# Layer 2's second fetch pass in a graph network kernel: four sums to a PSUM bank, a ring of 48 fetched tiles, and the node stage spread over three blocks

## The reference

```python
# layer 2, second relational convolution (per edge: its source's message in its relation)
msg = h[etype, src]                                   # rows of a table of node x relation
mean = segment_sum(msg, dst*8+etype) / max(cnt, 1)    # so each edge has a coefficient
x = x + mean.sum(over relations) + h @ root2 + b2
# layer 3, per node, before its edges are walked
nodes = relu(layernorm(x))
q = nodes @ Wq + bq ; k = nodes @ Wk + bk ; v = nodes @ Wv + bv
```

## Time and profile before

| What | us |
|---|---|
| median of three runs | 6053.4 |
| profiled execution, first to last instruction | 7221.2 |
| POOL busy in it | 4096.8 |
| TensorE busy | 4312.1 |
| VectorE busy | 3856.8 |
| this stage's fetches, first issue to last | 4527.5 to 5708.4 |
| the next stage's first fetch | 5748.0 |

### The profile page before, as it was taken

How to read it: one execution, slowest core, us unless ns; L and a number is a source line. 1 busy time by engine, 2 the same in 40 slices (tenths; PEclk the granted TensorE clock), 3 DMA queues, 4 the chain that set the end, 5 groups by cost and what they waited for, 6 DMA issues and landing times. The chain is left out here.

```text
span 7221.2 us, 86037 instructions
## 1 busy us (share of the span) xinstructions
PE 4312.1 (60%) x19030; PEld 3495.4 (48%) x19030; DVE 3856.8 (53%) x11927; ACT 1462.0 (20%) x3928; POOL 4096.8 (57%) x4194
## 2 busy tenths in 40 slices
PE   4577777846656565795666666333344446556565
PEld 4466666635555555443444444233333345555554
DVE  7344444446666556745555555244444446556665
ACT  4122222212222222361111111000000112222222
POOL 1566666646666565006666665666666556555653
PEclk9877767666666666897888888555655566676766
DMA  2433333323333334164444445122222433333333
GB/s 49 125 99 101 100 100 101 100 89 105 106 108 108 105 108 87 64 279 140 130 136 128 136 129 117 52 55 61 59 56 59 72 100 107 110 113 105 113 115 64
DMA packets 426871, 738.64 MB, mean 102 GB/s; under 512 B 100571, under 2 KB 280628, under 8 KB 419797
## 3 DMA queue, kind: packets, MB, share of 16 engines
q0 software_dynamic: 173296, 436.67, 23.0%
q1 hardware_dynamic: 244484, 289.62, 12.3%
q10 hardware_dynamic: 8592, 6.82, 0.4%
HBM read 613.74 MB, written 120.20 MB: 102 GB/s over the span
## 5 line engine op out<-in xcount | busy, mean ns | idle before, releaser
L1619 POOL DMA_INDIRECT xh<-pair_d,src_i x1658 | 1653.2, 997 | 1181.9 <-issue 457.1
L2630 POOL DMA_INDIRECT l2e_rows<-msg_d,msg_i x829 | 807.1, 974 | 744.7 <-POOLq L61 316.8
L986 POOL DMA_INDIRECT l0e_rows<-node_d,src_i x832 | 793.9, 954 | 465.0 <-issue 220.6
L841 POOL DMA_INDIRECT l2f_rows<-msg_d,msg_i x829 | 787.0, 949 | 428.4 <-issue 231.2
L1141 PE MATMUL l0e_ps<-l0e_rows,l0e_sel 128*128 128x256 f32 x1664 | 787.1, 570 | 304.1 <-issue 187.3
L875 PE MATMUL l2f_ps<-l2f_rows,l2f_sel 128*128 128x128 f32 x1664 | 403.8, 409 | 597.2 <-DVE xh L906 482.6
L2748 PE MATMUL l2e_ps<-l2e_rows,l2e_sel 128*128 128x256 f32 x1664 | 485.8, 424 | 423.2 <-DVE l2e_sel L2842 406.4
L875 PEld LDWEIGHTS l2f_ps<-l2f_rows,l2f_sel 128*128 128x128 f32 x1664 | 359.1, 304 | 671.3 <-issue 409.6
L2807 DVE TENSOR_TENSOR l_acc<-l_acc,l2e_ps 128x256 f32 x832 | 349.2, 420 | 511.5 <-DMA node_d<-l1t_queries 347.7
L1206 DVE TENSOR_TENSOR early_acc<-early_acc,l0e_ps 128x264 f32 x832 | 356.6, 429 | 470.7 <-PE l0e_ps L1142 181.6
L906 DVE TENSOR_TENSOR xh<-xh,l2f_ps 128x128 f32 x832 | 238.2, 286 | 676.3 <-DMA tb_raw<-edges_d,starti 466.7
(11 more groups left out here) (454 smaller groups left out, 8155.1 us busy)
## 6 DMA issues: line engine op xcount, KB each, us to landing
l0e_rows<-in_edge_attr_dram SPq DMA_DIRECT2D x832, 64.0 KB
msg_d<-l1t_queries SPq DMA_DIRECT2D x50, 1024.0 KB, 3.9
l1te_local<-local_d SPq DMA_DIRECT2D x52, 512.0 KB
l2e_local<-local_d SPq DMA_DIRECT2D x52, 512.0 KB
l3te_local<-local_d SPq DMA_DIRECT2D x52, 512.0 KB
xh<-pair_d,src_i POOLq DMA_INDIRECT x1658
msg_d<-l2e_msg SPq DMA_DIRECT2D x50, 512.0 KB
l0e_rows<-node_d,src_i POOLq DMA_INDIRECT x832
```

The costliest lines, as they stand in the source:

```text
L841: pool.indirect_dma_start(rows[:, t % R, :], None, table, bass.IndirectOffsetOnAxis(index[:, t:t + 1], 0)) \
L986: pool.indirect_dma_start(rows[:, t % R, 0:D], None, table, bass.IndirectOffsetOnAxis(g.src_i[:, t:t + 1], 0)).then_inc(gathered[t % R], 16)
L1619: pool.indirect_dma_start(rows[:, t % R, :], None, g.pair_d, bass.IndirectOffsetOnAxis(g.src_i[:, t:t + 1], 0)).then_inc(gathered[n % RG], 16)
L2630: pool.indirect_dma_start(rows[:, t % R, :], None, table, bass.IndirectOffsetOnAxis(index[:, t:t + 1], 0)).then_inc(gathered[t % R], 16)
```

## The change

In `gather_nodes` alone:

- The ring has 48 slots instead of 32.
- The four products of a group go side by side into one PSUM bank. There are still six banks, so PE may be 24 tiles ahead of the adds instead of six. `summed` is incremented once for a group and not once for a tile.
- Selections are made five groups ahead of the adds (six buffers) instead of two (four buffers).
- The node stage is spread out: `turn` comes six blocks behind the sums, `project` seven and `add_bias` eight, where all stood four behind. ACT's `move` trails its `norm` by two windows, and SP's `store` its loop by four. `scales` and `join` stay four blocks behind. After the last sum six `add_bias` are left (windows 44 to 49) instead of three (47 to 49).

```diff
@@ gather_nodes
-    R = 32
     G = 4
+    R = 48
+    RG = R // G
     B = 6
-    V = 4
+    AHEAD = B - 1
+    N = T // G
+    TURN, PROJECT, BIAS = 6, 7, 8
...
-        sel = st.sb("sel", [P, V, G, P])
+        sel = st.sb("sel", [P, B, G, P])
...
+        def landed(n):
+            return 16 * (G * (n // RG) + min(G, MOST - n * G))
...  POOL
-                        pool.wait_ge(summed, t - R + G)
+                        pool.wait_ge(summed, n - RG + 1)
...  SP
-                    if k >= 1:
-                        nodes.store(sp, k - 1)
-                nodes.store(sp, NW - 1)
+                    if k >= 4:
+                        nodes.store(sp, k - 4)
+                for k in range(NW - 4, NW):
+                    nodes.store(sp, k)
...  ACT
-                    nodes.move(act, k)
+                    if k >= 2:
+                        nodes.move(act, k - 2)
+                nodes.move(act, NW - 2)
+                nodes.move(act, NW - 1)
...  PE
-                for t in range(T):
-                    n, i, r = t // G, t // S, t % S
-                    if t % G == 0:
-                        pe.wait_ge(sel_made, n + 1)
-                        if t < MOST:
-                            pe.wait_ge(gathered[n % (R // G)], 16 * (G * (n // (R // G)) + min(G, MOST - t)))
-                    if t % 2 == 0 and t >= B:
-                        pe.wait_ge(added, t - B + 2)
-                    nc.tensor.matmul(ps[t % B][:, 0:D], sel[:, n % V, t % G, :], rows[:, t % R, :],
-                                     start=True, stop=True).then_inc(summed, 1)
-                    if i >= 4 and r == 8:
-                        nodes.turn(pe, i - 4)
-                    if i >= 4 and r == 12:
-                        nodes.project(pe, i - 4, first=i == 4)
-                for k in range(NS - 4, NW):
-                    nodes.turn(pe, k)
+                for n in range(N):
+                    i, q = n // (S // G), n % (S // G)
+                    pe.wait_ge(sel_made, n + 1)
+                    if n >= B:
+                        pe.wait_ge(added, G * (n - B + 1))
+                    if n * G < MOST:
+                        pe.wait_ge(gathered[n % RG], landed(n))
+                    for j in range(G):
+                        mm = nc.tensor.matmul(ps[n % B][:, j * D:(j + 1) * D], sel[:, n % B, j, :], rows[:, n % RG * G + j, :],
+                                              start=True, stop=True)
+                    mm.then_inc(summed, 1)
+                    if i >= TURN and q == 0:
+                        nodes.turn(pe, i - TURN)
+                    if i >= PROJECT and q == 2:
+                        nodes.project(pe, i - PROJECT, first=i == PROJECT)
+                for k in range(NS - PROJECT, NW):
+                    if k >= NS - TURN:
+                        nodes.turn(pe, k)
                     nodes.project(pe, k)
...  DVE
-                    if t % 2 == 0:
-                        dve.wait_ge(summed, t + 2)
+                    dve.wait_ge(summed, n + 1)
...
+                    if q == 0 and i >= BIAS:
+                        nodes.add_bias(dve, i - BIAS, first=i == BIAS)
                     if q == 1 and i >= 4:
                         nodes.scales(dve, i - 4)
                     if q == 2 and i >= 4:
                         nodes.join(dve, i - 4)
-                    if q == 3 and i >= 4:
-                        nodes.add_bias(dve, i - 4, first=i == 4)
-                for k in range(NS - 4, NW):
-                    nodes.scales(dve, k)
-                    nodes.join(dve, k)
+                for k in range(NS - BIAS, NW):
+                    late = {NS - BIAS: NW - 2, NS - BIAS + 2: NW - 1}.get(k)
+                    if late is not None:
+                        nodes.scales(dve, late)
+                        nodes.join(dve, late)
                     nodes.add_bias(dve, k)
```

More of the change, by code:

```diff
@@ L819, in gather_nodes @@
 def gather_nodes(nc, g, sem, name, table, index, coef, weights, biases, scale, queries):
-    R = 32
     G = 4
+    R = 48
+    RG = R // G
     B = 6
-    V = 4
+    AHEAD = B - 1
+    N = T // G
+    TURN, PROJECT, BIAS = 6, 7, 8
     with Stage(nc, name) as st:
         rows = st.sb("rows", [P, R, D])
-        sel = st.sb("sel", [P, V, G, P])
+        sel = st.sb("sel", [P, B, G, P])
         ps = [st.ps(f"ps{b}") for b in range(B)]
         nodes = Nodes(nc, g, sem, st, name, weights, biases, False, scale, queries)
-        gathered = [sem(f"{name}_g{r}") for r in range(R // G)]
+        gathered = [sem(f"{name}_g{r}") for r in range(RG)]
         sel_made, summed, added = sem(name + "_sel"), sem(name + "_summed"), sem(name + "_added")
+        def landed(n):
+            return 16 * (G * (n // RG) + min(G, MOST - n * G))
         with nc.Block() as block:
@@ L839, in _ @@
                     if t >= R and t % G == 0:
-                        pool.wait_ge(summed, t - R + G)
+                        pool.wait_ge(summed, n - RG + 1)
                     pool.indirect_dma_start(rows[:, t % R, :], None, table, bass.IndirectOffsetOnAxis(index[:, t:t + 1], 0)) \
-                        .then_inc(gathered[n % (R // G)], 16)
+                        .then_inc(gathered[n % RG], 16)
             @block.sync
@@ L889, in make_sel @@
                 def make_sel(n):
[L890 to L894, removed]
+                    if n >= B:
+                        dve.wait_ge(summed, n - B + 1)
+                    for j in range(G):
+                        t = n * G + j
+                        ins = nc.vector.tensor_scalar(sel[:, n % B, j, :], g.iota[:, :], g.dloc[:, t:t + 1],
@@ L895, in make_sel, with add @@
                                                       coef[:, t:t + 1], ALU.is_equal, ALU.mult)
                     ins.then_inc(sel_made, 1)
[L898 to L901, removed]
-                    if t % 2 == 0:
-                        dve.wait_ge(summed, t + 2)
-                    if t >= 1:
-                        dve.wait_ge(added, t)
-                    nc.vector.tensor_tensor(x, x, ps[t % B][:, 0:D], ALU.add).then_inc(added, 1)
+                def add(n):
+                    if n % (S // G) == 0:
+                        windows[:] = windows_of(nc, g, mybir.EngineType.DVE, n * G, S)
+                    dve.wait_ge(summed, n + 1)
+                    for j in range(G):
+                        t = n * G + j
+                        x = nodes.x_of(windows[t % S])
+                        if t >= 1:
+                            dve.wait_ge(added, t)
+                        nc.vector.tensor_tensor(x, x, ps[n % B][:, j * D:(j + 1) * D], ALU.add).then_inc(added, 1)
@@ L908, in _ @@
                 nodes.prepare(dve)
-                make_sel(0)
-                make_sel(1)
-                for n in range(T // G):
+                for n in range(AHEAD):
+                    make_sel(n)
+                for n in range(N):
                     i, q = n // (S // G), n % (S // G)
[L913 to L916, removed]
+                    if n + AHEAD < N:
+                        make_sel(n + AHEAD)
+                    add(n)
+                    if q == 0 and i >= BIAS:
+                        nodes.add_bias(dve, i - BIAS, first=i == BIAS)
```

## The result

| | us |
|---|---|
| changed kernel, median of 14 runs | 6069.68 (6062.64 to 6073.74) |
| before, median of 14 runs beside it | 6053.91 |
| ratio | 1.0023, 95% interval [1.0016, 1.003] |
| profiled execution of the changed kernel: its run, its span | 6067.42, 6065.4 |

So the change costs 15.8 us by the medians and 13.9 by the ratio, which leaves out one run of before that took 14346.8 us in a slow state; the interval is 9.7 to 18.2 us. The forecast was 6059 with a range of 6030 to 6074.

The account below looks back on a forecast made before the run. The prediction took POOL's fetch issue, 1.25 us each, to bound the stage, with nearly all stalls due to the profile. Its terms, 9.3 + 0.9 - 4 = +6, gave 6059 us, range 6030 to 6074.

Parts of the forecast that it names:

- Bound by POOL's issue, stalls from the recording: Stage's fetches: POOL issues one per 1.25 us; nearly all of its 147 us of stalls come with the profile.
- fetched data are hardly ever what PE waits for: PE's waits in the stage: only 14.7 us are for fetched data, at the start.
- rival A: Stage's stalls are real, up to 147 us, and deeper buffers remove them: 5916 us at most, 5990 with half; chance 0.2.
- span down and median not: Profile afterwards: span shorter by up to 147 less 10 with median unmoved would prove the stalls come with the profile.
- The end of the stage: From last add to next stage: 22.1 us instead of 12.8, so +9.3, with six windows of bias adds left.
- The bias adds' stores in the body hidden: Node stage in the body: stores that `add_bias` waits for land within 3.3 us, against two groups (10 us) of room.
- The last group, +0.9: Last group's adds start behind four products instead of two: +0.9 us taken, between -0.7 and +0.9.
- The gain of 4 us in the body: Deeper ring, banks and selections remove stalls in the measured time: between 0 and 9 us, 4 taken.
- the 75 us between the median and the stall-free sum: Whole kernel: 5978 us without any stall, 75 below the median; this stage's share 147/1243, about 9 us.
- it lies beside POOL's 5.0 us a group: PE's waits on adds and one DVE wait per group are hidden: DVE needs 3.0 us of POOL's 5.0.
- the forecast's own 6056 to 6066: Whole kernel's time: the interval of the prediction's main case, with chance 0.42.
- rival B: End of stage dearer: six windows by the store's chain at 3.1 us, no stall to win, +12.6, 6066 to 6076; chance 0.18.

Follow-up runs that it names:

- second recording: The kernel before, unchanged, profiled once more: its run took 6046.91 us, its span is 6044.7 us.
- disturbed recording: The profiled execution of the kernel before that the prediction was read from, nothing changed: span 7221.2 us.

## Why the prediction was right or wrong

- **Bound by POOL's issue, stalls from the recording: right.** The second recording shows it, and a ring of 16 confirms it. Not right was "fetched data are hardly ever what PE waits for": undisturbed, PE starts a group 2.6 us after its last fetch is issued, with a median landing of 2.5, so the fetch is what it waits for. The rule of the Trainium skill, "Perfetto Trace Analysis", section "Tensor Engine Instruction (MATMUL, LD_WEIGHTS)", on estimated ends of matmuls, which spoke for rival A, isn't needed: the 7.65 us delay has gone with the disturbed recording, and the second has none over 1.4 us. The sign "span down and median not" came out, but the span fell by 1155.8 us, since the new recording was not disturbed; so it says nothing of depth, on which the rings of 16 and 48 decide.
- **The end of the stage: right, in size too.** +9.3 was worked out, +9.0 measured. From the last add the key and value adds ended at 2.2, 6.6, 11.8, 14.3, 16.8 and 19.2 us; the steps had 2.5, 5.0, 11.7, 14.2, 16.7 and 19.2. One step was missing: window 45 waited 1.82 us for the store of 44. It cost nothing, since 46 was held by the `keep` anyway; the `keep` was issued at 8.0, as worked out.
- **The bias adds' stores in the body hidden: right.** Two waits for stores in the whole stage, both behind the last add.
- **The last group, +0.9: mis-sized.** Last issue to last add grew by 0.2.
- **The gain of 4 us in the body: wrong, the step that failed.** It shared the 75 us between the median and the stall-free sum among the stages by the stalls of the first recording. There were none here to remove. In the second recording the five walks take 1065.2, 1061.6, 1049.8, 1035.9 and 1061.9 us from first issue to last, 89 us more than 1.25 us a fetch, and all of it is in the four others. All else takes 770 us there, not 793; the late landings of padding are in that part and not in the 75. Where the 89 lie (busy us, mean ns of one, idle us; L1619 is two walks):

```profile
L1619 POOL DMA_INDIRECT xh<-pair_d,src_i x1658 | 1617.6, 976 | 571.4 <-issue 491.0
L2630 POOL DMA_INDIRECT l2e_rows<-msg_d,msg_i x829 | 798.5, 963 | 567.7 <-POOLq L61 315.5
L986 POOL DMA_INDIRECT l0e_rows<-node_d,src_i x832 | 791.8, 952 | 282.2 <-issue 221.6
L841 POOL DMA_INDIRECT l2f_rows<-msg_d,msg_i x829 | 784.5, 946 | 288.7 <-issue 241.7
```

By the means against 946 ns, longer fetches are about 50, 14 and 5 us of it, and in the first walk (L986) POOL waits 52.7 us for PE in 104 times, some 21 us more than the 0.30 that any fetch has. Spreading a surplus by the stalls of the disturbed recording gave this stage a share that it does not have.

In place of the gain stood a loss of 2 to 3 us: "it lies beside POOL's 5.0 us a group" counted VectorE's time and not that its selections hold up POOL's issue. (The working also starts from 20 selections ahead of the first add instead of 8; the kernels make 24 and 12. The difference, 12, is the same.)

- **The total.** The stage grew by 12.2 instead of 6.2: 7.0 from the body (4 not gained, 3.0 lost), less 0.7 and 0.3 for the two end terms. The time is inside the range, 4 us below its upper bound, and outside of the forecast's own 6056 to 6066. By its size it is where rival B stood, but not by B's way: no window went by the store's chain of 3.1 us. So the range held it by luck: its upper part was there for a mechanism that did not come. The ratio is just over the bound of 0.2%, which lies inside its interval, and slower had a chance of 0.19 only; with the body's term at zero or above the sum would have been 10 to 13 and the chances of same and slower near each other.

## What to carry to other kernels

Look at the span of the recording before its waits: where it is 19% above the median, the same kernel recorded again is worth more than any argument from its stalls. Depth (rings, banks, work made ahead) is worth nothing where the issuing engine never waits, while steps that are moved past the last input are paid for: here 6.2 us for three windows, and 2.8 more because on SP's queue a large store stood ahead of a small one that was waited for. Count what lies between the last issue and its use: here it was 17.9 us, more than the whole change costs, and 10.3 of them went with another padding index.

## What the runs showed of the hardware

- An indirect fetch of 128 rows of 512 bytes that all read one row lands late when such fetches follow each other: up to 9.2 us (10.6 in the changed kernel) instead of the median of 2.5. Sources of 128 different rows take the longest down to 3.5, and the kernel by 42 us. Whether memory or the DMA engines hold them was not tested.
- VectorE's selections of 128x128 lengthen some of GpSimd's indirect DMA issues from 0.94 to as much as 1.07 us: in the changed kernel 41 fetches are over 1 us, 16 with the same four selections between adds, and one with three of the four left out.
